# A graph network on one core: the segment maxima read their penalties from PSUM in pieces, and the adding transfers are shared out anew over the stages

## The chip, the cores and the metric

The kernel runs on one NeuronCore of one Trainium2 chip. The metric is the device time in microseconds (us) of one launch. Three runs of the kernel before took 6823.45, 6824.31 and 6814.25 us; their median is 6823.45 us.

The engines are named as in the profile: PE (TensorE matmul), PEld (its weight load), DVE (VectorE), ACT (ScalarE), POOL (GpSimd) and SP (SyncE, which here only issues transfers). A name with a q behind it (ACTq, SPq, POOLq, PEq) is that engine's sequencer.

## The reference, cut to what matters

The program is a stack of four graph layers on 6250 nodes and 106250 edges, sorted by target node. The first is a pair of attention convolutions (GATv2), the first with 8 heads of 16 channels and the second with 1 head of 64:

```
def _gatv2_layer(x, src, dst, Wl, bl, Wr, br, att, bias, heads, out_ch, concat):
    xl = (x @ Wl + bl).reshape(N, heads, out_ch)
    xr = (x @ Wr + br).reshape(N, heads, out_ch)
    e = jax.nn.leaky_relu(xl[src] + xr[dst], NEG_SLOPE)
    logits = jnp.einsum('ehc,hc->eh', e, att)
    m = jax.ops.segment_max(logits, dst, num_segments=N)
    ex = jnp.exp(logits - m[dst])
    denom = jax.ops.segment_sum(ex, dst, num_segments=N)
    alpha = ex / denom[dst]
    msg = xl[src] * alpha[..., None]
    out = jax.ops.segment_sum(msg, dst, num_segments=N)
...
_gatv2_layer(..., heads=8, out_ch=16, concat=True), then elu
_gatv2_layer(..., heads=1, out_ch=64, concat=False), then elu
```

The change touches `m`, the segment maxima of the two layers. The three layers behind (a normalised convolution, one with edge attributes and batch norms, and three more convolutions) are not changed. They read a dense adjacency matrix in DRAM, into which the kernel adds the edge weights while the two attention layers run.

## The kernel before, in words

**Stages.** The program is a row of stages. Each has all engines at work side by side and ends in a barrier of all engines (`S.end_stage()`, in the profile line L89): each engine drains, POOL collects the others, clears the semaphores and releases them. So a stage lasts as long as its slowest engine or transfer. An attention layer (`gat_layer`) has, in this order, the dense products (`two_dense`), the logits of all edges (`gat_logits`), the segment maxima (`edge_max`) and the weighted sums (`gat_sums`).

**Tiles.** The edges are cut into 880 tiles of 128 and these into 220 groups of 4. `gat_logits` writes the logits of every group to DRAM (`heads`), `edge_max` reads them all back, and `gat_sums` runs a software pipeline over the 220 groups.

**Segment maxima.** In `edge_max` the logits lie in one array `run` of 128 partitions by L columns, each partition with a consecutive stretch of edges (of one head, in layer 1): L is 7040 with 8 heads and 880 with one. A running maximum within each segment is one DVE scan, `state = max(state + penalty, value)`, where the penalty is 0 within a segment and -BIG where a new one starts. It is made forwards with the penalties `opens` and then backwards with `closes`, each time twice: once without what comes from the neighbouring partitions, then `carried` works out what crosses the partitions' borders (four small matmuls of PE and small DVE steps), and the scan is made again with it. The penalties are bf16 and lie in SBUF. ScalarE sums them once each (`sum_pens`), as `carried` needs the sum of each partition's penalties. Before that, `load_pens` has ScalarE's queue issue the loads: `opens` at once, and `closes` only after the first transfers of `opens` have landed and VectorE is through with `own_logits`, whose data lies where `closes` goes. `own_logits` is VectorE's work on the self loops, ahead of the scans. The results go back to DRAM in two transfers of SP, one for each half of the columns.

**Adding transfers.** `merge(groups)` is POOL's work beside the stages: for each of 150 groups of tiles, 4 indirect transfers that add edge weights into the adjacency matrix. Each of these transfers is one POOL instruction (DMA_INDIRECT, L1108). Two groups may be in flight: group n waits until group n-2 has landed, and where the blocks of both clash also until group n-1 has. Whether they clash is a number in the table `CLEAR`, which POOL's sequencer loads into a register ahead of each group (L1100). `MERGES` sets how many groups stand in which stage, for layer 1 and for layer 2: after the gathers of the logits, in the maxima, in the sums, and beside the work that follows. Each stage's barrier waits for all of its groups.

Of the kernel before, what the change touches and what calls it, by code (L numbers as in the profile page):

```python
# [7 lines left out]
ALU = mybir.AluOpType  # L8
ACT = mybir.ActivationFunctionType
# [10 lines left out]
P = 128  # L20
# [44 lines left out]
MERGES = ((2, 5, 64, 9), (2, 3, 54, 11))  # L65
# [65 lines left out]
def gnn(nc, A, out):  # L131
    S = Sems(nc)
    ve, ac, pe, po, sp = nc.vector, nc.scalar, nc.tensor, nc.gpsimd, nc.sync
    with ExitStack() as ctx:
# [958 lines left out]
        def merge(groups):  # L1093


            for n in range(sent[0], min(sent[0] + groups, FAR)):
                g, own, other = merge_turn(n), merged[n % 2], merged[(n + 1) % 2]
                wait(po, own, 16 * GT * (n // 2))
                if n > 2:
                    clear_at = nc.values_load(CLEAR[0:1, n - 1:n], engines=(POOL,), min_val=16 * GT,  # L1100
                                              max_val=16 * GT * FAR,
                                              skip_runtime_bounds_check_because="a count of transfers of groups")
                    po.wait_ge(other, clear_at)
                elif n:
                    po.wait_ge(other, 16 * GT)
# [841 lines left out]
        def edge_max(H, C, XL, XR, self_l):  # L1947
# [7 lines left out]
            assert L % 2 == 0  # L1955
            unread = G[:, :, :, :].rearrange("p r t d -> p (r t d)").bitcast(BF16)[:, 0:L // 2]
# [21 lines left out]
            sums_of_pens = [ends[:, 4 + i:5 + i] for i in range(4)]  # L1978
# [17 lines left out]
            def sum_pens():  # L1996

                ac.wait_ge(S("opens1"), 16 * H)
                for i, cols in enumerate(HALVES):
                    wait(ac, S("pens"), i)  # L2000
                    ac.activation(unread, opens[:, cols], ACT.Copy, accum_out=sums_of_pens[i]).then_inc(S("pens"), 1)
                ac.wait_ge(S("closes"), 16 * H)
                for i, cols in enumerate(HALVES):
                    ac.wait_ge(S("pens"), 2 + i)
                    ac.activation(unread, closes[:, cols], ACT.Copy, accum_out=sums_of_pens[2 + i]).then_inc(S("pens"), 1)

            def carried(flip):

                last = run[:, 0:1] if flip else run[:, L - 1:L]
                ve.wait_ge(S("pens"), 2 + 2 * flip)  # L2010
                go(ve, lambda: ve.tensor_tensor(ends[:, 1:2], sums_of_pens[2 * flip], sums_of_pens[2 * flip + 1], ALU.add))
# [3 lines left out]
                with ExitStack() as ps:  # L2015
                    lines = psum(ps, "lines", [P, 3 * P])
                    for n in range(2):
                        go(pe, lambda: pe.matmul(lines[0:1, n * P:(n + 1) * P], ends[:, n:n + 1], ident[:, :],
                                                 start=True, stop=True))
                    go(ve, lambda: ve.tensor_copy(row[0:1, 0:2 * P], lines[0:1, 0:2 * P]))  # L2020

                    start = chunks - 1 if flip else 0
                    first = [r.rearrange("a (h c) -> a h c", h=H)[:, :, start] for r in (penalty, carry)]
                    go(ve, lambda: ve.memset(first[0], -BIG))
                    turn = (lambda r: r[:, ::-1]) if flip else (lambda r: r)
                    go(ve, lambda: ve.tensor_tensor_scan(turn(state), turn(penalty), turn(value), -BIG,
                                                         ALU.add, ALU.max))
                    if flip:
                        go(ve, lambda: ve.tensor_copy(carry[:, 0:P - 1], state[:, 1:P]))
                    else:  # L2030
                        go(ve, lambda: ve.tensor_copy(carry[:, 1:P], state[:, 0:P - 1]))
                    go(ve, lambda: ve.memset(first[1], -BIG))
                    go(pe, lambda: pe.matmul(lines[:, 2 * P:2 * P + 1], carry, ones[0:1, 0:1], start=True, stop=True))
# [745 lines left out]
```

## Time and profile before

| | |
|---|---|
| median of 3 runs | 6823.45 us (6814.25 to 6824.31) |
| span of the profiled execution, first to last instruction | 6814.5 us |
| the profiled execution's own time | not given beside its span; the nearest run is 6814.25 us |
| POOL, DVE, PE, ACT busy | 68%, 55%, 82%, 32% of the span |
| L1108, adding transfers on POOL | 600 instructions, 1025.6 us busy |
| segment maxima of layer 1 | 1313.5 to 1417.8 us |
| sums of layer 1 | 1417.8 to 1921.5 us |
| segment maxima of layer 2 | 3158.3 to 3191.7 us |
| sums of layer 2 | 3191.7 to 3603.8 us |

Times within the trace count from the start of the span. A row of the timeline gives the start, the duration, the engine, the line, the operation with what it writes and reads, how many equal instructions it stands for, and in brackets how long the engine was idle before it and what ended that. A matmul's end is modelled; issuing, register, branch and semaphore instructions are not counted as busy. A stage's end is read off the first instruction of the next.

### The profile page before, as it was taken

To read this page: it belongs to the slowest core of one execution; us is meant where nothing else is said; L and a number is where in the kernel's file an instruction comes from. 1 tells how busy PE (TensorE), PEld (TensorE's weight loads), DVE (VectorE), ACT (ScalarE), POOL (GpSimd) and SP (SyncE) were. 2 spreads that over 40 slices of the span, in tenths; PEclk is the share of its full clock that TensorE was granted. 3 is DMA by queue.
4 is the path that set the end of the run, shared out by engine and by line. 5 is a ranking of instruction groups with operands and counts; after the bars stand their busy time and mean duration, and the time that the engine had idled before them with its cause. 6 is when DMAs were issued, how large, how long until landed. Compare 5 with 4: busy or idle time off the path is not lost. (4 is left out here: it accounts for less than half of the span.)

```text
span 6814.5 us, 123136 instructions
## 1 busy us (share of the span) xinstructions
PE 5620.4 (82%) x35774; PEld 4535.0 (67%) x35774; DVE 3761.5 (55%) x13008; ACT 2152.8 (32%) x6966; POOL 4663.4 (68%) x4391
## 2 busy tenths in 40 slices
PE   2999999557759999886886996666666599999999
PEld 2788888546657787775775996666666455555555
DVE  6555552389945555224887445666666544344343
ACT  4333334269923333333994003222222300000000
POOL 1777777688877777777887661777777267376473
PEclk9899999779969999997997998999999799999999
DMA  5888865656734444335444884555555389898997
GB/s 198 266 280 283 281 202 158 121 116 147 144 37 103 101 105 103 81 80 61 76 76 128 288 288 138 159 158 158 158 158 158 52 291 306 294 306 301 304 305 262
DMA packets 904054, 1232.19 MB, mean 181 GB/s; under 512 B 230601, under 2 KB 640861, under 8 KB 890407
## 3 DMA queue, kind: packets, MB, share of 16 engines
q1 hardware_dynamic: 607544, 887.00, 40.5%
q0 software_dynamic: 207392, 219.55, 17.6%
q10 hardware_dynamic: 88428, 117.57, 5.1%
q8 instruction: 295, 4.83, 0.3%
q14 instruction: 395, 3.24, 0.1%
HBM read 987.45 MB, written 237.38 MB: 180 GB/s over the span
## 5 line engine op out<-in xcount | busy, mean ns | idle before, releaser
L1024 POOL DMA_INDIRECT ACC<-table,TABS x1760 | 1701.3, 967 | 587.9 <-issue 583.3
L1346 POOL DMA_INDIRECT BUF<-table,TABS x840 | 797.5, 949 | 596.1 <-issue 245.4
L1108 POOL DMA_INDIRECT adjacency<-TABS x600 | 1025.6, 1709 | 247.8 <-issue 206.2
L1024 POOL DMA_INDIRECT BUF<-table,TABS x880 | 836.9, 951 | 331.3 <-issue 331.3
L1803 PE MATMUL picked<-ident,ACC 128*128 128x128 f32 (+1 forms) x3520 | 716.5, 287 | 0.0
L2169 PE MATMUL asum<-BUF 128*128 128x144 f32 x3520 | 544.5, 298 | 171.2 <-DVE BUF L2147 168.9
L1879 DVE SCALAR_TENSOR_TENSOR BUF<-BUF,TABS,wspread 128x128 bf16<-128x128 f32 (+1 forms) x600 | 323.9, 540 | 644.3 <-issue 625.6
L2169 PEld LDWEIGHTS asum<-BUF 128*128 128x128 f32 x3520 | 461.7, 192 | 202.4 <-issue 196.5
L2115 ACT ACTIVATE BUF<-iota_row,TABS 128x128 f32<-128x128 f32 x1760 | 555.1, 386 | 68.6 <-PEq L89 68.6
L1796 PE MATMUL picked<-ident 128*128 128x128 f32 x3520 | 565.2, 309 | 9.7 <-PEq L89 9.7
L1802 PE MATMUL picked<-G,OH 128*128 128x128 f32 (+1 forms) x2352 | 495.5, 295 | 84.3 <-DMA ACC<-table,TABS 70.1
L1718 PE MATMUL sums<-BUF,OH 128*128 128x128 f32 x1760 | 253.5, 288 | 361.9 <-DVE BUF L1704 361.8
L1796 PEld LDWEIGHTS picked<-ident 128*128 128x128 f32 x3520 | 475.5, 210 | 107.0 <-issue 106.8
L1823 PEld LDWEIGHTS lcol<-attT,BUF 128*128 128x128 f32 (+1 forms) x3520 | 433.2, 192 | 143.5 <-issue 141.6
L1803 PEld LDWEIGHTS picked<-ident,ACC 128*128 128x128 f32 (+1 forms) x3520 | 523.7, 177 | 0.0
L1054 DVE TENSOR_TENSOR ACC<-ACC,asum 128x144 f32 (+1 forms) x1760 | 462.1, 263 | 84.5 <-issue 10.1
L1829 ACT ACTIVATE ACC<-lcol 128x32 f32<-128x32 f32 (+1 forms) x440 | 81.7, 186 | 1281.0 <-PE lcol L1823 1267.8
L1718 PEld LDWEIGHTS sums<-BUF,OH 128*128 128x128 f32 x1760 | 217.6, 194 | 396.5 <-issue 396.4
L1823 PE MATMUL lcol<-attT,BUF 128*128 128x8 f32 (+1 forms) x3520 | 456.4, 252 | 2.7 <-ACT BUF L1841 2.7
L1815 DVE TENSOR_TENSOR BUF<-BUF,picked 128x512 f32<-128x512 f32 (+1 forms) x440 | 297.2, 676 | 230.8 <-ACT BUF L1809 230.7
L1802 PEld LDWEIGHTS picked<-G,OH 128*128 128x128 f32 (+1 forms) x2352 | 343.9, 178 | 118.4 <-issue 71.6
L1779 DVE TENSOR_SCALAR G<-BUF,iota_col 128x512 f32<-128x512 bf16 x440 | 219.2, 498 | 359.2 <-DMA BUF<-locals 355.1
(409 smaller groups left out, 10909.1 us busy)
## 6 DMA issues: line engine op xcount, KB each, us to landing
TABS<-adjacency SPq DMA_DIRECT2D x272, 512.0 KB
BUF<-in_edge_pair SPq DMA_DIRECT2D x880, 128.0 KB
BUF<-adjacency SPq DMA_DIRECT2D x102, 1024.0 KB
BUF<-adjacency SPq DMA_DIRECT2D x204, 512.0 KB, 5.1
adjacency<-zeros ACTq DMA_DIRECT2D x44, 1792.0 KB
G<-adjacency SPq DMA_DIRECT2D x136, 512.0 KB
kept<-ACC SPq DMA_DIRECT2D x220, 272.0 KB
G<-kept SPq DMA_DIRECT2D x220, 272.0 KB
```

The costliest lines, as they stand in the source:

```text
L1024: po.indirect_dma_start(rows[:, slot, j, 0:width], None, tab, bass.IndirectOffsetOnAxis(ap=SRC[:, q * GT + j:q * GT + j + 1], axis=0)).the ...
L1054: ve.tensor_tensor(at, at, self.from_[:, j, 0:self.width], ALU.add).then_inc(S("added"), 1)
L1108: po.indirect_dma_start(adj_flat, bass.IndirectOffsetOnAxis(ap=PLACE[:, k:k + 1], axis=0), TOTAL[:, k:k + 1], None, compute_op=ALU.add).th ...
L1346: po.indirect_dma_start(R[:, q % deep_ring, j, :], None, table, bass.IndirectOffsetOnAxis(ap=SRC[:, k:k + 1], axis=0)).then_inc(S(f"gather ...
L1718: m = pe.matmul(sums[h][:, j, :], OH[:, h, j, :], V[:, q % 3, j, :], start=True, stop=True)
L1796: pe.matmul(picked[slot][:, j * P:(j + 1) * P], ident[:, :], ident[:, :], start=True, stop=True)
L1802: pe.matmul(z, XRB[q % 3][:, j, :], OHT[:, slot, j, :], start=True, stop=False)
L1803: m = pe.matmul(z, R[:, q % DEEP, j, :], ident[:, :], start=False, stop=True)
L1823: m = pe.matmul(lcol[slot % 2][:, j * H:(j + 1) * H], Z[:, q % 3, j * P:(j + 1) * P], attT[0:W, 0:H], start=True, stop=True)
L1879: ve.scalar_tensor_tensor(JUNK[:, at % 3, 0:j + 1, :], KEYS[:, n % 2, 0:j + 1, :], KEY[:, k:k + 1], wspread[:, 0:j + 1, :], ALU.is_equal, ...
L2115: ac.activation(HOT[:, slot, j, :], iota_row[:, :], ACT.Abs, scale=-1.0, bias=LOCAL[:, bass.ds(q * GT + j, 1)]).then_inc(S("gap"), 1)
L2169: m = pe.matmul(sums[slot % 2][:, j, 0:WIDE], HOT[:, slot, j, :], RHS[:, slot, j, :], start=True, stop=True)
```

## The change

There are three parts.

1. `edge_max` no longer scans with penalties in SBUF. ScalarE copies them in pieces into PSUM (`put_pens`), two buffers in turn, and each DVE scan reads one piece there (`scans`). There are 5 pieces of 1408 columns with 8 heads and 2 of 440 with one. Every penalty is read in two passes, so there are 20 copies and 20 scans in layer 1, where 4 summing passes and 6 scans stood, and 8 and 8 in layer 2. The copies of the passes without the carried values give the sums too. The semaphore `scanned` counts scans, and `pens` counts copies: copy n waits for scan n-2, scan n for copy n and scan n-1.
2. `MERGES`: of the 80 groups of layer 1, 10 instead of 5 stand in the maxima and 59 instead of 64 in the sums. Of the 70 of layer 2, 4 instead of 3 stand in the maxima and 53 instead of 54 in the sums.
3. In `merge` the register load of `CLEAR` is no longer told to skip its bounds check.

The core of the diff:

```diff
-MERGES = ((2, 5, 64, 9), (2, 3, 54, 11))
+MERGES = ((2, 10, 59, 9), (2, 4, 53, 11))
...
                     clear_at = nc.values_load(CLEAR[0:1, n - 1:n], engines=(POOL,), min_val=16 * GT,
-                                              max_val=16 * GT * FAR,
-                                              skip_runtime_bounds_check_because="a count of transfers of groups")
+                                              max_val=16 * GT * FAR)
                     po.wait_ge(other, clear_at)
...
-            assert L % 2 == 0
-            unread = G[:, :, :, :].rearrange("p r t d -> p (r t d)").bitcast(BF16)[:, 0:L // 2]
+            pieces = 5 if H > 1 else 2
+            size, room = L // pieces, 3 * 512
+            assert L % 2 == 0 and L % pieces == 0 and size <= room
...
-            sums_of_pens = [ends[:, 4 + i:5 + i] for i in range(4)]
+            sums_of_pens = [ends[:, 4 + i * pieces:4 + (i + 1) * pieces] for i in range(2)]
+            turns = [(flip, full, k) for flip in (False, True) for full in (False, True)
+                     for k in (reversed(range(pieces)) if flip else range(pieces))]
...
-            def sum_pens():
-
-                ac.wait_ge(S("opens1"), 16 * H)
-                for i, cols in enumerate(HALVES):
-                    wait(ac, S("pens"), i)
-                    ac.activation(unread, opens[:, cols], ACT.Copy, accum_out=sums_of_pens[i]).then_inc(S("pens"), 1)
...
+            def put_pens(pens):
+
+                for n, (flip, full, k) in enumerate(turns):
+                    if flip:
+                        ac.wait_ge(S("closes"), 16 * H)
+                    else:
+                        ac.wait_ge(S(f"opens{((k + 1) * size - 1) // (L // 2)}"), 16 * H)
+                    wait(ac, S("scanned"), n - 1)
+                    given = (closes if flip else opens)[:, k * size:(k + 1) * size]
+                    more = {} if full else {"accum_out": sums_of_pens[flip][:, k:k + 1]}
+                    ac.activation(pens[:, n % 2, 0:size], given, ACT.Copy, **more).then_inc(S("pens"), 1)
...
+            def scans(pens, lines):
+
+                for n, (flip, full, k) in enumerate(turns):
+                    turn = (lambda t: t[:, ::-1]) if flip else (lambda t: t)
+                    at = slice(k * size, (k + 1) * size)
+                    data, pen = turn(run[:, at]), turn(pens[:, n % 2, 0:size])
...
+                    wait(ve, S("scanned"), n)
+                    ve.wait_ge(S("pens"), n + 1)
+                    if full and at_end:
+                        ve.wait_ge(chain[0].sem, chain[0].n)
+                    ve.tensor_tensor_scan(data, pen, data, initial, ALU.add, ALU.max).then_inc(S("scanned"), 1)
+                    if not full and k == (0 if flip else pieces - 1):
+                        ve.wait_ge(S("scanned"), n + 1)
+                        carried(flip, lines)
+                    if flip and full and at.start <= L // 2 < at.stop or flip and full and not k:
+                        half = 1 if k else 0
+                        sp.wait_ge(S("scanned"), n + 1)
+                        sp.dma_start(in_dram[:, HALVES[half]], run[:, HALVES[half]]).then_inc(S("maxima"), 16)
...
             load_pens()
-            sum_pens()
-            scans()
+            with ExitStack() as ps:
+                pens = psum(ps, "pens", [P, 2, room])
+                lines = psum(ps, "lines", [P, 3 * P])
+                put_pens(pens)
+                scans(pens, lines)
```

`carried` does what it did; its first step now sums 5 (or 2) columns of `sums_of_pens` instead of two.

Three places show how the instructions stand. The first is ScalarE in the maxima of layer 1, before, with the two loads ahead; `pool4` to `pool7` are semaphores, which stand for `opens0`, `opens1`, `closes` and `pens` there.

```order
L1993 DMA BUF<-close_pen 16x7040 [waits pool1,pool4]
L1993 DMA BUF<-close_pen 16x7040 x7
L2001 ACTIVATE G,st<-BUF 128x3520 [waits pool5]
L2001 ACTIVATE G,st<-BUF 128x3520 [waits pool7]
L2005 ACTIVATE G,st<-BUF 128x3520 [waits pool7,pool6]
L2005 ACTIVATE G,st<-BUF 128x3520 [waits pool7]
```

And now, where `pool7` is `scanned`:

```order
L1995 DMA BUF<-close_pen 16x7040 [waits pool1,pool4]
L1995 DMA BUF<-close_pen 16x7040 x7
L2008 ACTIVATE pens,st<-BUF 128x1408 [waits pool4] x2
L2008 ACTIVATE pens,st<-BUF 128x1408 [waits pool7,pool5] x3
L2008 ACTIVATE pens<-BUF 128x1408 [waits pool7,pool4] x2
L2008 ACTIVATE pens<-BUF 128x1408 [waits pool7,pool5] x3
L2008 ACTIVATE pens,st<-BUF 128x1408 [waits pool7,pool6] x5
L2008 ACTIVATE pens<-BUF 128x1408 [waits pool7,pool6] x5
```

The first copy stands behind the 8 loads of `closes`, and 20 copies stand where 4 passes stood.

The second is VectorE there, from the last step of `own_logits` to the second forward pass, before (a scan is called SCALAR_TENSOR_TENSOR in this listing):

```order
L1976 TENSOR_REDUCE st<-BUF 128x120 [waits pool1]
L2040 SCALAR_TENSOR_TENSOR ACC<-BUF,ACC 128x3520 [waits pool1,pool4,pool2]
L2040 SCALAR_TENSOR_TENSOR ACC<-BUF,ACC 128x3520 [waits pool1,pool5,pool3]
L2011 TENSOR_TENSOR st<-st 128x1 [waits pool1,pool7]
L2012 COPY st<-ACC 128x1 [waits pool1]
```

And now, where `pool8` is the new `pens`:

```order
L2053 SCALAR_TENSOR_TENSOR ACC<-pens,ACC 128x1408 [waits pool8,pool2]
L2053 SCALAR_TENSOR_TENSOR ACC<-pens,ACC 128x1408 [waits pool8,pool7,pool2]
L2053 SCALAR_TENSOR_TENSOR ACC<-pens,ACC 128x1408 [waits pool8,pool7,pool3] x3
L2013 TENSOR_REDUCE st<-st 128x1 [waits pool1,pool7]
L2014 COPY st<-ACC 128x1 [waits pool1]
```

Each scan now waits for a copy of ScalarE, the first one included.

The third is POOL at the start of the maxima of layer 1, two of its groups before (L89 is the barrier):

```order
L89 ISA [waits barrier_Pool_Activation_PE_DVE_SP_gather]
L1108 DMA adjacency<-TABS 37748736x1 [waits merged_into_adjacency_0,merged_into_adjacency_1]
L1108 DMA adjacency<-TABS 37748736x1 x3
L1100 TENSOR_LOAD CLEAR [waits merged_into_adjacency_1]
L1108 DMA adjacency<-TABS 37748736x1 [waits merged_into_adjacency_0]
L1108 DMA adjacency<-TABS 37748736x1 x3
```

And now:

```order
L89 ISA [waits barrier_Pool_Activation_PE_DVE_SP_gather]
L1107 DMA adjacency<-TABS 37748736x1 [waits merged_into_adjacency_0,merged_into_adjacency_1]
L1107 DMA adjacency<-TABS 37748736x1 x3
L1100 TENSOR_LOAD CLEAR [waits merged_into_adjacency_1]
L1100 ISA x2
L1107 DMA adjacency<-TABS 37748736x1 [waits merged_into_adjacency_0]
L1107 DMA adjacency<-TABS 37748736x1 x3
```

Behind each of the 147 loads of `CLEAR` there are now two instructions of POOL's sequencer (ISA x2, asserts of the lower and upper bound) that were not there.

## Rows read from the trace of the kernel before

**Rows 1.** The page: busy time by engine, and the group of layer 1's gathers
```profile
PE 5620.4 (82%) x35774; PEld 4535.0 (67%) x35774; DVE 3761.5 (55%) x13008; ACT 2152.8 (32%) x6966; POOL 4663.4 (68%) x4391
L1024 POOL DMA_INDIRECT ACC<-table,TABS x1760 | 1701.3, 967 | 587.9 <-issue 583.3
```
**Rows 2.** Windows, the four stages: length, busy (count) by engine, PE clock, DMA share, GB/s
```profile
1313.50:1417.80 104.30, 3.50 (x12) 1.33 (x12) 91.15 (x34) 12.92 (x8) 86.81 (x20) 0.50 0.49 104
1417.80:1921.50 503.70, 349.80 (x2200) 299.07 (x2200) 431.61 (x1761) 422.82 (x1321) 420.02 (x256) 0.94 0.65 131
3158.30:3191.70 33.40, 3.50 (x12) 1.33 (x12) 25.50 (x26) 2.65 (x9) 25.16 (x12) 0.50 0.27 41
3191.70:3603.80 412.10, 338.58 (x2200) 293.63 (x2200) 342.08 (x1982) 402.71 (x1320) 338.21 (x216) 0.99 0.48 74
```
**Rows 3.** Timeline, end of layer 1's sums
```profile
1880.31 1.64 DVE L1054 TENSOR_TENSOR ACC<-ACC,asum 128x144 f32 x4 [0.23 <-DVE ACC L1054]
1881.13 1.55 POOL L1108 DMA_INDIRECT adjacency<-TABS  x1 [0.31 <-issue]
...
1916.44 1.55 POOL L1108 DMA_INDIRECT adjacency<-TABS  x1 [0.30 <-issue]
1921.51 0.56 DVE L2223 TENSOR_SCALAR st<-ACC 128x392 f32<-128x392 f32 x1 [39.56 <-PEq L89]
```
**Rows 4.** Timeline, end of layer 2's sums
```profile
3595.36 1.57 POOL L1108 DMA_INDIRECT adjacency<-TABS  x1 [0.31 <-issue]
...
3600.59 1.32 DVE L1054 TENSOR_TENSOR ACC<-ACC,asum 128x67 f32 x4 [0.31 <-DVE ACC L1054]
3603.84 0.21 DVE L2223 TENSOR_SCALAR st<-ACC 128x49 f32<-128x49 f32 x1 [1.93 <-PEq L89]
```
**Rows 5.** Timeline, layer 1's maxima
```profile
1338.99 2.17 POOL L1108 DMA_INDIRECT adjacency<-TABS  x1 [5.01 <-DMA adjacency<-TABS]
...
1342.00 3.61 ACTq L1993 DMA_DIRECT2D BUF<-close_pen  x8
1342.05 15.18 DVE L2040 TENSOR_TENSOR_SCAN ACC<-BUF,ACC 128x3520 f32<-128x3520 bf16 x2
1343.32 7.58 POOL L1108 DMA_INDIRECT adjacency<-TABS  x1 [0.30 <-issue]
1345.65 3.14 ACT L2001 ACTIVATE G<-BUF 128x3520 bf16<-128x3520 bf16 x1 [35.98 <-issue]
...
1361.22 14.88 DVE L2043 TENSOR_TENSOR_SCAN ACC<-BUF,st,ACC 128x7040 f32<-128x7040 bf16 x1
1362.61 14.86 POOL L1108 DMA_INDIRECT adjacency<-TABS  x1 [0.30 <-issue]
...
1402.62 7.55 DVE L2049 TENSOR_TENSOR_SCAN ACC<-BUF,ACC 128x3520 f32<-128x3520 bf16 x1
1404.25 7.28 POOL L1108 DMA_INDIRECT adjacency<-TABS  x1 [0.30 <-issue]
```
**Rows 6.** Timeline, layer 2's maxima
```profile
3172.31 1.55 POOL L1108 DMA_INDIRECT adjacency<-TABS  x1 [0.30 <-issue]
3172.63 0.57 ACT L2001 ACTIVATE G<-BUF 128x440 bf16<-128x440 bf16 x1 [16.21 <-DVE st L1976]
...
3186.34 1.57 POOL L1108 DMA_INDIRECT adjacency<-TABS  x1 [0.31 <-issue]
...
3187.94 1.13 DVE L2049 TENSOR_TENSOR_SCAN ACC<-BUF,ACC 128x440 f32<-128x440 bf16 x1
```
**Rows 7.** Timeline, layer 1's logits: a DVE operation that reads PSUM, and POOL
```profile
1267.48 0.67 DVE L1815 TENSOR_TENSOR BUF<-BUF,picked 128x512 f32<-128x512 f32 x1
1267.61 0.94 POOL L1024 DMA_INDIRECT ACC<-table,TABS  x1 [0.30 <-issue]
```
**Rows 8.** The same operation with both inputs in SBUF (layer 2's dense products)
```profile
1968.35 0.69 DVE L885 TENSOR_TENSOR BUF<-BUF 128x512 f32<-128x512 f32 x1
```
**Rows 9.** Line L1100: count, shortest/median/longest in ns
```profile
L1100 POOLq TENSOR_LOAD <-CLEAR x147: 283/288/309, 1315.3 to 3674.5; - x147
```

More of the change, by code:

```diff
@@ L2014, in carried @@
                 state, carry = row[0:1, 2 * P:3 * P], st[2][0:1, 0:P]
[L2015 to L2029, printed above, removed]
-                    else:
-                        go(ve, lambda: ve.tensor_copy(carry[:, 1:P], state[:, 0:P - 1]))
-                    go(ve, lambda: ve.memset(first[1], -BIG))
-                    go(pe, lambda: pe.matmul(lines[:, 2 * P:2 * P + 1], carry, ones[0:1, 0:1], start=True, stop=True))
-                    go(ve, lambda: ve.tensor_copy(ends[:, 2:3], lines[:, 2 * P:2 * P + 1]))
@@ L2036, in scans @@
-            def scans():
-                for i, cols in enumerate(HALVES):
-                    ve.wait_ge(S(f"run{i}"), 16)
-                    ve.wait_ge(S(f"opens{i}"), 16 * H)
-                    go(ve, lambda: ve.tensor_tensor_scan(run[:, cols], opens[:, cols], run[:, cols],
-                                                         run[:, L // 2 - 1:L // 2] if i else -BIG, ALU.add, ALU.max))
-                carried(False)
-                go(ve, lambda: ve.tensor_tensor_scan(run, opens, run, ends[:, 2:3], ALU.add, ALU.max))
-                ve.wait_ge(S("closes"), 16 * H)
-                go(ve, lambda: ve.tensor_tensor_scan(run[:, ::-1], closes[:, ::-1], run[:, ::-1], -BIG, ALU.add, ALU.max))
-                carried(True)
-                for i in (1, 0):
-                    data, pen = (t[:, HALVES[i]][:, ::-1] for t in (run, closes))
-                    go(ve, lambda: ve.tensor_tensor_scan(data, pen, data, ends[:, 2:3] if i else run[:, L // 2:L // 2 + 1],
-                                                         ALU.add, ALU.max))
-                    sp.wait_ge(chain[0].sem, chain[0].n)
-                    sp.dma_start(in_dram[:, HALVES[i]], run[:, HALVES[i]]).then_inc(S("maxima"), 16)
@@ new lines, in carried @@
+                for n in range(2):
+                    go(pe, lambda: pe.matmul(lines[0:1, n * P:(n + 1) * P], ends[:, n:n + 1], ident[:, :],
+                                             start=True, stop=True))
+                go(ve, lambda: ve.tensor_copy(row[0:1, 0:2 * P], lines[0:1, 0:2 * P]))
+                start = chunks - 1 if flip else 0
+                first = [r.rearrange("a (h c) -> a h c", h=H)[:, :, start] for r in (penalty, carry)]
+                go(ve, lambda: ve.memset(first[0], -BIG))
```

25 lines of the change are left out of this document (18 added, 7 removed).

## The prediction

> **What bounds the kernel now.** I read the page first. POOL is busy 68% of the span and PE 82% [rows 1], but the kernel is a row of stages with a barrier behind each, so shares decide nothing. I went on to the windows of the four stages that the change touches [rows 2], then to the timeline at each one's end, to see who is last there.
>
> Sums of layer 1, 503.7 us: DVE's last add ends at 1880.31 + 1.64 = 1881.95, PE's matmuls are done before it, and POOL goes on alone with adding transfers, one every 1.86 us, until 1916.44 + 1.55 = 1917.99. DVE sits idle for 39.56 us [rows 3]. POOL bounds this stage. From POOL's last end to the next stage it is 1921.51 - 1917.99 = 3.5 us.
>
> Sums of layer 2, 412.1 us: POOL's last transfer ends at 3596.93 and DVE's last add at 3601.91; the next stage starts 1.9 us after DVE [rows 4]. The pipeline bounds it. POOL with its 3.5 us would have been through at 3600.4, so it has 3.4 us of slack.
>
> Maxima of layer 1, 104.3 us: a chain of DVE. The scans end at 1402.62 + 7.55 = 1410.17 [rows 5], and the last result transfer and the barrier take the 7.6 us to 1417.8. In it POOL does 20 transfers only: a transfer started beside a scan takes 7.58, 14.86 and 7.28 us instead of 1.55, and ends 1.4 us after the scan does (1362.61 + 14.86 = 1377.47 against 1376.10) [rows 5]. The scans shut it out. Maxima of layer 2, 33.4 us: DVE ends at 3189.07, POOL at 3187.91 [rows 6], next stage 3191.7.
>
> **Part 1, the groups taken from layer 1's sums.** 5 groups are 20 transfers. The last 20 began at 1881.13 (the 18 left out in rows 3 repeat the pattern), so the 236 that stay would end at 1880.8, and POOL would let the barrier go at 1880.8 + 3.5 = 1884.3. The pipeline would do so at 1881.95 + 1.9 = 1883.9. The two are level, and what is late next is both. The stage shrinks from 503.7 to 466.5 us: **-37.2 us**. The pace over the whole stage gives the same: 256 transfers in 500.2 us are 1.95 each, and 236 of them 461, to 1879.
>
> **Part 2, scans by pieces in layer 1.** Three terms on DVE's chain.
> (a) The first scan began at 1342.05, just behind own_logits. Now it needs a copy, and ScalarE first issues 8 loads of closes, which hold it until 1345.65 [rows 5]. ScalarE takes 3.14 us for 3520 columns and 0.57 for 440 [rows 5, 6], so 0.834 ns a column and 0.20 fixed: 1.38 us for 1408. With some 0.15 for reading out the sum and for the semaphore the scan starts at 1347.2: **+5.1**.
> (b) A scan takes 7.55 us for 3520 columns and 1.13 for 440, so 2.085 ns a column and 0.21 fixed: 3.15 for 1408. 20 of them with about 0.12 between (two scans with a wait between take 15.18, not 15.10; those with waits on two further semaphores a little more) are 65.3 us. The six of before took 68.12 less the two carried steps of 4.0 = 60.1. **+5.2**. The copy (1.5) lies beside the scan before it (3.15), since two buffers are there. closes, issued by 1345.6, is first needed at about 1380, 34 us later; opens, as large, was there 28 us after its issue.
> (c) The barrier: POOL's last transfer ended at 1404.25 + 7.28 = 1411.53, and with it in the way the next stage came 7.6 us behind the scans. POOL is now done earlier; I take **-1** for it.
> Together **+9.3 us**, if POOL gets through its 40 transfers. It has begun 10 before 1343.32 (that row is its eleventh) as before; the other 30 at 1.95 take 58.5 us, to 1402. The loads of opens delayed a landing until 1338.99, a stall of 5.01 [rows 5]; closes, as large, may cost such a stall again: 1407. The scans end at 1420.5 and the next stage starts at 1427.1; POOL, with its 3.5, may take until 1423.6. There are 17 us of cover.
>
> **Does a scan with one input in PSUM leave POOL alone?** Rows 7: L1815 reads PSUM and SBUF, POOL's transfer starts 0.13 us into it with 0.54 to go, and takes 0.94. Shut out, it would have taken 0.54 and then, as behind the scans, 1.4. Over all 1760 gathers the mean is 0.967 [rows 1], though an L1815 of 0.68 runs beside every few of them, so hardly one was held. I take it that such a scan does leave POOL alone.
> The Trainium skill says the same as a mechanism (SBUF — State Buffer, "SBUF: two separate sides"): VectorE and GpSimd share one pair of ports, an exclusive lock that a DVE operation takes with two SBUF inputs or in a two-port mode and holds to its end. The scans of before agree (14.86 us beside 14.88).
>
> **What a PSUM read costs.** The trace has no scan from PSUM. The nearest rows: 128x512 with PSUM takes 0.67 and with both in SBUF 0.69 [rows 7, 8]. I take no difference for the 28 scans; the lower end is no gain either.
> A rule speaks against it: the Trainium skill (VectorE: DVE Perf Modes, "The TRN2 errata") has VectorE's fixed part at 120 cycles from PSUM against 58 from SBUF, which by its 0.96 GHz is an estimate of 0.065 us a scan, 1.3 us for 20. Rows 7 and 8 do not show it.
> The upper end is a copy that doesn't lie beside its scan: 1.5 us for each of 19 further pieces, +28.5 (rival C).
>
> **Part 3, layer 2's maxima.** On DVE, the first copy starts at 3172.63 [rows 6] and the scan at 3173.35, 1.05 later; 8 scans of 1.13 + 0.12 are 10.0 against 8.85 (3172.30 to 3189.07 less two carried steps): +2.2, which would have the next stage at 3193.9. POOL has 16 transfers instead of 12. The fifth began at 3172.31, and 12 at 1.86 from there end at 3194.3; with the 3.5 us of rows 3 behind them the next stage starts at 3197.8. POOL becomes the last: 3197.8 - 3191.7 = **+6.1 us**. (Before, 12 transfers ended at 3187.91, and DVE's scans held some of them: 8 took 15.6 us instead of 14.9.)
>
> **Part 4, layer 2's sums.** One group fewer on POOL, which isn't the bound: **0**. The 9 and 11 groups behind the sums stay.
>
> **Part 5, the asserts.** 147 pairs on POOL's sequencer. A CLEAR load (0.288 us) [rows 9] stands ahead of each group too, and every gap between transfers is 0.30 us [rows 3], a group's first or not: the sequencer works ahead of the engine. Taken at 0. Above: each assert as long as that load and not hidden, 0.58 us a group.
>
> **The sum** against the execution's span: -37.2 + 9.3 + 6.1 + 0 = -21.8, 6814.5 to 6792.7. The span is level with the fastest run (6814.25) and 9 us under the median, and the difference is what carries over: 6823.45 - 21.8 = **6801.7 us**.
>
> **Rivals.**
> A. The scans go on shutting POOL out (the port is held all the same). For: POOL's stretched transfers [rows 5] say nothing of the reason. Against: rows 7. Then one transfer goes with each scan: 10 + 20 + 4 in the carried steps = 34 by the end of the scans at 1420.5, and 6 more at 1.86 with the 1.4 behind the scan and the drain end the stage at 1436, 18.2 over before. Layer 2's maxima, with a transfer or two held, about +7.5. -37.2 + 18.2 + 7.5 = -11.5: 6812 us.
> B. The asserts are not hidden, and the kernel gets slower. Place: POOL's queue ahead of each group. At 0.58 us a pair: layer 1's sums +34.2 on a POOL-bound stage, layer 2's maxima +2.3, layer 2's sums 53 x 0.58 = 30.7 less the slack, which is 3.4 and the group taken away, 7.4: +19.9. In all +56.4 - 21.8 = +34.6: 6858 us. With p us a pair it is 116 p - 10.8 - 21.8: it eats the gain from 0.28 us a pair, and shows as slower from 0.40. Against it: the gaps of rows 3.
> C. The hand-over between ScalarE and VectorE is serial (PSUM can't be written and read at once, or the semaphores cost more than I think). Layer 1 +28.5; layer 2's scans 7 x 0.67 = 4.7, of which POOL hides all but 0.8. +29.3 - 21.8 = +7.5: 6831 us. For: nothing in this trace has ScalarE write PSUM while VectorE reads it. Against: they use different parts of PSUM, and PE writes PSUM while DVE reads in every pipeline here.
>
> **How the numbers follow.** Forecast 0.74, A 0.08, B 0.06, C 0.12. A measurement of this kernel tells about 0.2% (13.6 us) from no change: below 6809.8 is faster, above 6837.1 slower. The forecast's own spread is some 9 us (stalls for landings in the maxima, the pace in the sums, which of the runs' levels from 6814 to 6824 holds), so nearly all of it is faster. C is the same at full price and in part faster; A just so. Faster 0.78, same 0.15, slower 0.07. The range runs from 6788, below the forecast, to 6816, which takes in A and the cheaper part of C.
>
> **What would show it.** Right: in the sums of layer 1 DVE's idle time before L2234 (the old L2223) falls from 39.56 to under 5 us; the stage is 466 us. In layer 1's maxima 40 transfers of POOL, those beside the scans at 1.55 to 2 us; 20 scans of 3.15; the first at 5 us behind own_logits; a stage of 113 to 114 us. In layer 2's maxima POOL is last, 39.5 us. Gaps between transfers stay 0.30. Wrong: transfers of 3 us beside the scans (A), gaps of 0.6 or more ahead of each group's first transfer (B), scans 4.5 us apart (C).

## The result, and the profile after

The changed kernel takes 6811.51 us (median of 20 runs, 6798.93 to 6826.45) against 6823.66 us of the kernel before (20 runs, 6812.41 to 6836.07). The ratio is 0.9983, 95% interval 0.9978 to 0.9989: 11.6 us less, with 7.5 and 15.0 as ends (the two medians differ by 12.2). Forecast were 21.8 us less, 6801.7 us. The direction and the place were right, and the size was half of what I forecast.

The profiled execution took 6799.69 us for a span of 6797.9, so the launch adds 1.8 us to a span. It is the second fastest of the 20. The windows of the same four stages as in [rows 2], with the same columns:

```profile
1317.50:1429.50 112.00, 3.50 (x12) 1.33 (x12) 94.17 (x48) 28.05 (x30) 67.31 (x40) 0.50 0.53 97
1429.50:1899.40 469.90, 357.07 (x2200) 305.78 (x2200) 432.40 (x1761) 422.84 (x1321) 387.29 (x236) 0.95 0.71 140
3134.00:3172.80 38.80, 3.51 (x12) 1.33 (x12) 25.88 (x28) 4.71 (x13) 30.18 (x16) 0.50 0.29 35
3172.80:3584.70 411.90, 341.19 (x2200) 296.06 (x2200) 341.27 (x1982) 402.87 (x1320) 331.85 (x212) 0.98 0.50 74
```

They are 1032.6 us against 1053.5, so 20.9 less: +7.7, -33.8, +5.4, -0.2. The forecast had +9.3, -37.2, +6.1 and 0.

The end of layer 1's sums, where [rows 3] had DVE idle for 39.56 us (L2234 is the old L2223, L1107 the old L1108):

```profile
1889.55 1.55 POOL L1107 DMA_INDIRECT adjacency<-TABS  x1 [0.30 <-issue]
...
1897.09 1.65 DVE L1054 TENSOR_TENSOR ACC<-ACC,asum 128x144 f32 x4 [0.23 <-DVE ACC L1054]
...
1899.51 0.56 DVE L2234 TENSOR_SCALAR st<-ACC 128x392 f32<-128x392 f32 x1 [0.77 <-PEq L89]
```

POOL is through at 1891.10 and DVE at 1898.74. The pipeline bounds the stage now, and the 36 us that POOL had for itself are gone.

Layer 1's maxima, the stretch that answers to [rows 5]:

```profile
1343.83 2.15 DVE L1976 TENSOR_REDUCE st<-BUF 128x120 f32<-128x1920 f32 x1
...
1346.07 3.61 ACTq L1995 DMA_DIRECT2D BUF<-close_pen  x8
...
1349.73 1.35 ACT L2008 ACTIVATE pens<-BUF 128x1408 f32<-128x1408 bf16 x1 [35.97 <-issue]
1349.75 1.55 POOL L1107 DMA_INDIRECT adjacency<-TABS  x1 [0.30 <-issue]
...
1351.30 16.06 DVE L2053 TENSOR_TENSOR_SCAN ACC<-pens,ACC 128x1408 f32<-128x1408 f32 x5 [5.31 <-ACT pens L2008]
1351.61 1.55 POOL L1107 DMA_INDIRECT adjacency<-TABS  x1 [0.30 <-issue]
...
1371.38 3.15 DVE L2053 TENSOR_TENSOR_SCAN ACC<-pens,st,ACC 128x1408 f32<-128x1408 f32 x1
...
1374.62 28.74 DVE L2053 TENSOR_TENSOR_SCAN ACC<-pens,ACC 128x1408 f32<-128x1408 f32 x9
1374.62 1.35 ACT L2008 ACTIVATE pens<-BUF 128x1408 f32<-128x1408 bf16 x1 [5.83 <-DVE ACC L2053]
1374.72 1.55 POOL L1107 DMA_INDIRECT adjacency<-TABS  x1 [0.31 <-issue]
...
1406.31 1.55 POOL L1107 DMA_INDIRECT adjacency<-TABS  x1 [0.31 <-issue]
...
1407.38 3.15 DVE L2053 TENSOR_TENSOR_SCAN ACC<-pens,st,ACC 128x1408 f32<-128x1408 f32 x1
1410.57 12.71 DVE L2053 TENSOR_TENSOR_SCAN ACC<-pens,ACC 128x1408 f32<-128x1408 f32 x4
```

Three things are to be seen. The first scan waits 5.31 us for the first copy, which stands behind the 8 loads of closes. Nine scans take 28.74 us, 3.19 each with the hand-over, and each later copy (1.35) lies beside a scan. POOL's transfers take 1.55 us in the middle of scans and follow each other at 1.86; the last of the 40 ends at 1407.86, 21.6 us ahead of the next stage.

In layer 2's maxima POOL is last:

```profile
3165.13 1.13 DVE L2053 TENSOR_TENSOR_SCAN ACC<-pens,ACC 128x440 f32<-128x440 f32 x1
...
3168.46 1.57 POOL L1107 DMA_INDIRECT adjacency<-TABS  x1 [0.30 <-issue]
3172.79 0.40 ACT L2126 ACTIVATE BUF<-iota_row,TABS 128x128 f32<-128x128 f32 x1 [12.20 <-PEq L89]
```

The line of the bounds check shows what the asserts are:

```profile
L1100 POOLq TENSOR_LOAD <-CLEAR x147: 283/288/306, 1319.4 to 3655.4; - x147
L1100 POOLq FUSED_REGOPS  x147: 147/147/181, 1319.7 to 3655.7; - x147
L1100 POOLq SEQ_ASSERT  x147: 18/18/28, 1320.0 to 3655.9; - x147
```

Each group costs POOL's sequencer 0.165 us more (0.147 and 0.018), while the gaps between transfers stay at 0.30.

### The profile page after: what moved, and what is told of

It reads as the page before. It is cut to its first block and busy times, and to the rows that moved or that the text cites. A ratio compares the mean times of both kernels' runs of the same rounds, so it can differ in the third digit from the quotient of the medians.

```text
span 6797.9 us, 123518 instructions
## 1 busy us (share of the span) xinstructions
PE 5630.2 (83%) x35774; PEld 4544.0 (67%) x35774; DVE 3768.0 (55%) x13024; ACT 2169.8 (32%) x6992; POOL 4606.4 (68%) x4391
## 3 DMA queue, kind: packets, MB, share of 16 engines
q0 software_dynamic: 207392, 219.55, 18.4%
## 5 line engine op out<-in xcount | busy, mean ns | idle before, releaser
L1107 POOL DMA_INDIRECT adjacency<-TABS x600 | 971.7, 1619 | 285.3 <-issue 242.4
```

The source lines that it names most:

```text
L1107: po.indirect_dma_start(adj_flat, bass.IndirectOffsetOnAxis(ap=PLACE[:, k:k + 1], axis=0), TOTAL[:, k:k + 1], None, compute_op=ALU.add).th ...
```

## The experiments

The runs fell into three batches, each on one chip and with its own runs of the kernel before. On the chips of batch 1 and batch 3 this kernel is slower: the kernel before takes 8391.83 and 8353.17 us there (medians), and the mean granted clock is 0.821 to 0.830 in the profiled executions, where it was 0.935 for [rows 2]. Batch 2 was on a chip like the first (6815.58 us). Across the chips the maxima repeat to some 0.4 us and layer 2's sums to 2, so they can be compared; layer 1's sums move by up to 11 us for one and the same kernel. The time of the slower chips goes into stages that the change doesn't touch, above all the logits. A ratio is always against the kernel before in the same batch. All lengths, from barrier to barrier in us:

```
                         maxima 1  sums 1  maxima 2  sums 2 |  four   | logits 1
before                    104.31   503.67   33.35    412.12 | 1053.45 | 1141.01
after                     111.99   469.93   38.80    411.89 | 1032.61 | 1146.08
asserts_again (batch 2)   104.33   502.54   33.36    412.90 | 1053.13 | 1139.60
padded (batch 2)          104.01   503.60   33.35    411.88 | 1052.84 | 1140.48
sbuf_pieces (batch 2)     118.48   472.13   40.71    410.97 | 1042.29 | 1139.93
best (batch 2)            106.90   470.71   33.57    411.95 | 1023.13 | 1143.33
asserts_only (batch 1)    104.38   497.60   33.37    412.18 | 1047.53 | 1632.27
scans_only (batch 1)      112.16   494.49   35.28    411.61 | 1053.54 | 1652.04
merges_only (batch 1)     139.19   476.27   40.49    410.99 | 1066.94 | 1635.05
a_again (batch 1)         111.99   480.68   38.81    411.01 | 1042.49 | 1656.02
a_third (batch 3)         111.99   472.52   38.82    411.00 | 1034.33 | 1628.10
scans_again (batch 3)     111.99   498.86   34.90    412.04 | 1057.79 | 1635.39
early_copies (batch 3)    106.79   480.54   38.84    412.64 | 1038.81 | 1640.36
```

**asserts_only.** The kernel before with part 3 of the change alone.

```diff
-                                              max_val=16 * GT * FAR,
-                                              skip_runtime_bounds_check_because="a count of transfers of groups")
+                                              max_val=16 * GT * FAR)
```

> The kernel before with the bounds check of the register load (part 3 alone). My theory (hidden, since POOL's sequencer works ahead of the engine): gaps between transfers stay 0.30 us, the four stages last 104, 504, 33 and 412 us, whole kernel 0 +- 3 us. Rival (an assert costs as the load before it, 0.29 us, twice and not hidden): layer 1's sums 504 + 64 x 0.58 = 541 us and the whole kernel 50 us slower.

Measured: ratio 1.0005 (0.9990 to 1.0019), with the maxima and layer 2's sums of the old lengths. Layer 1's sums take 497.60 us, 6 less than before and not more. The gap ahead of a group's first transfer there is 0.30 us (median), as between the others. The asserts are hidden; rival B is out.

**scans_only.** The changed kernel with the old groups.

```diff
-MERGES = ((2, 10, 59, 9), (2, 4, 53, 11))
+MERGES = ((2, 5, 64, 9), (2, 3, 54, 11))
```

> The changed scans and asserts with the old shares of adding transfers (5, 64, 9 and 3, 54, 11). My theory (only the moved transfers gain, and the scans cost): layer 1's maxima 112 us (+7.7), POOL idle in them early; layer 1's sums stay bound by POOL at 504 us; layer 2's maxima bound by VectorE at 35.5 us (+2.2). Whole kernel +10 us, 6833. Rival (the scans from PSUM gain by themselves, as scan and POOL no longer hold each other up): no more than the time of before, 6823 or less.

Measured: 1.0012 (0.9998 to 1.0025). The maxima are 112.16 and 35.28 us: the scans by pieces cost 7.8 and 1.9 us and bring nothing by themselves. Layer 1's sums are 494.49 us, not the 504 expected, and POOL is last there still (see below).

**merges_only.** The kernel before with parts 2 and 3.

```diff
-MERGES = ((2, 5, 64, 9), (2, 3, 54, 11))
+MERGES = ((2, 10, 59, 9), (2, 4, 53, 11))
```

> The old scans with both inputs in SBUF, with the new shares of adding transfers (10, 59 and 4, 53) and the asserts. My theory (the scans shut POOL out): layer 1's maxima hold 20 further transfers that start only behind the scans, 20 x 1.86 us and 3.5 us to the next stage: about 139 us (+34); the sums 469 us (-34); layer 2's maxima 39.5 us (+6). Whole kernel +6 us, 6830. Rival (the shares alone make the gain, and POOL finds room in the stage anyway): layer 1's maxima 105 us, whole kernel 6795 to 6800.

Measured: slower, 1.0022 (1.0006 to 1.0038), 18 us (5 to 32) where 6 were expected. The maxima came as expected, 139.19 us; layer 1's sums are 476.27 instead of 469. The window and POOL's last transfer of that stage:

```profile
1806.07:1945.26 139.19, 3.50 (x12) 1.33 (x12) 91.16 (x34) 12.92 (x8) 116.80 (x40) 0.50 0.43 78
```
```profile
1940.25 1.55 POOL L1107 DMA_INDIRECT adjacency<-TABS  x1 [0.30 <-issue]
1945.76 0.40 ACT L2114 ACTIVATE BUF<-iota_row,TABS 128x128 f32<-128x128 f32 x1 [88.21 <-PEq L89]
```

POOL works on to 1941.8, long after the scans, which had shut it out. What the sums give back (21.3 us against asserts_only) is more than eaten. So the new groups don't pay beside the long scans of before, and the scans by pieces don't pay without the new groups.

**a_again.** The changed kernel unchanged, in the same batch.

> The changed kernel once more, unchanged, for a second trace of it. Theory N (what the four changed stages gain is fixed, and the rest of the difference to the whole program's time is drift of stages that the change doesn't touch, with the phase of TensorE's clock): the four stages last 112, 470, 38.8 and 412 us again within 2 us each, some 21 us less than before in sum, while the untouched stages move by up to 5 us each in either direction between traces. Theory S (the change itself makes other stages slower): the layer 1 logits last 1146 us again as in the first trace of the changed kernel, 5 us more than before. Whole kernel: ratio 0.998.

Measured: 0.9992 (0.9981 to 1.0003), 6.7 us less, which is not clear of no change. The maxima repeat to 0.01 us. The sums of layer 1 do not, against the expectation of 470 within 2: 480.68 us.

**sbuf_pieces.** The pieces and groups of the changed kernel, but ScalarE copies the penalties to SBUF (into G, as bf16).

```diff
-                pens = psum(ps, "pens", [P, 2, room])
+                pens = G[:, :, :, :].rearrange("p r t d -> p (r t d)").bitcast(BF16)[:, 0:2 * size].rearrange(
+                    "p (a n) -> p a n", a=2)
```

> The changed kernel, with ScalarE's pieces written as bf16 into SBUF instead of f32 into PSUM: the same 20 copies and 20 scans, the same shares of transfers, but both inputs of a scan in SBUF. My theory (it is the place of the penalties that frees POOL): a transfer begun beside a scan lasts to the scan's end, one goes with each scan, 34 of 40 are through when the scans end, and 6 more at 1.86 us end layer 1's maxima at about 122 us; layer 2's at 40 us. Rival (short scans with gaps between are enough to let POOL through): 112 and 38.8 us as in the changed kernel. The scans themselves 3.15 us in both, if a read from PSUM costs nothing more.

```profile
1342.95 1.55 POOL L1107 DMA_INDIRECT adjacency<-TABS  x1 [0.30 <-issue]
...
1344.38 16.06 DVE L2053 TENSOR_TENSOR_SCAN ACC<-G,ACC 128x1408 f32<-128x1408 bf16 x5 [5.31 <-ACT G L2008]
1344.81 4.02 POOL L1107 DMA_INDIRECT adjacency<-TABS  x1 [0.30 <-issue]
...
1349.13 2.94 POOL L1107 DMA_INDIRECT adjacency<-TABS  x1 [0.30 <-issue]
...
1352.38 2.94 POOL L1107 DMA_INDIRECT adjacency<-TABS  x1 [0.30 <-issue]
```

What changed is where the penalties lie, and with it their type (bf16, as before the change, instead of f32). The scans take the same (five in 16.06 us, as from PSUM), and POOL's transfers beside them take some 2.9 us, and one 4.02, instead of 1.55: about one for each scan. 35 of the 40 are through when the scans end; 34 were expected. Maxima 118.48 us instead of 111.99. Two findings: a scan with both inputs in SBUF holds POOL up and one with an input in PSUM doesn't, and reading PSUM costs the scan nothing.

Ratio 0.9984 (0.9975 to 0.9993), which the timed runs can't tell from the changed kernel's 0.9983. So cutting the scans is what turns the loss of merges_only into a gain, since a transfer gets in between two pieces: 139.19 us become 118.48. PSUM brings the other 6.5 us in layer 1's maxima and 1.9 in layer 2's (40.71 to 38.80), seen in the stages alone. Not tested is a kernel that cuts the scans and reads the penalties where they lie, without any copy. It would have no first copy to wait for.

The Trainium skill (VectorE: DVE Perf Modes, "The TRN2 errata") would make the 20 scans from PSUM 1.3 us longer, an estimate from its fixed cycles; the two rows of 16.06 us do not show it. Its rule on the shared ports (SBUF — State Buffer, "SBUF: two separate sides") is borne out as far as VectorE holds POOL up: with two SBUF inputs it does, with one it doesn't. The other direction, POOL's transfer holding up a scan, is not to be seen here: the transfers of 2.94 us end 1.27 us into the next scan, and that scan still takes 3.15 us.

**best.** The changed kernel with ScalarE's first two copies issued ahead of the loads of closes, and layer 2's groups put back.

```diff
-MERGES = ((2, 10, 59, 9), (2, 4, 53, 11))
+MERGES = ((2, 10, 59, 9), (2, 3, 54, 11))
...
-            def load_pens():
+            def load_pens(pens):
...
+                put_pens(pens, 0, 2)
...
-                for n, (flip, full, k) in enumerate(turns):
+                for n, (flip, full, k) in list(enumerate(turns))[first:last]:
...
-                put_pens(pens)
+                load_pens(pens)
+                put_pens(pens, 2, len(turns))
```

> The changed kernel with two edits: ScalarE makes its first two copies before it issues the loads of closes, and layer 2 has its old shares (3 and 54). My theory (the first scan's 5.1 us wait is the queue of ScalarE, and in layer 2's maxima the fourth group makes POOL the last): VectorE's first scan starts right behind own_logits; layer 1's maxima 112 - 5.1 = 107 us; layer 2's 35.3 - 1.05 = 34.2 us; the sums as they were, 412 us in layer 2. The four stages 9.7 us less than in the changed kernel. Rival (closes is then late, or copies during own_logits hold its operations): layer 1's maxima stay at 110 us or more.

```profile
1335.56 1.35 ACT L2009 ACTIVATE pens<-BUF 128x1408 f32<-128x1408 bf16 x1 [24.09 <-DMA BUF<-open_pen]
...
1341.57 2.15 DVE L1976 TENSOR_REDUCE st<-BUF 128x120 f32<-128x1920 f32 x1
1343.32 1.55 POOL L1107 DMA_INDIRECT adjacency<-TABS  x1 [0.31 <-issue]
1343.63 16.05 DVE L2054 TENSOR_TENSOR_SCAN ACC<-pens,ACC 128x1408 f32<-128x1408 f32 x5
1343.81 3.61 ACTq L1996 DMA_DIRECT2D BUF<-close_pen  x8
```

Measured: 6786.08 us (6779.82 to 6795.90, 5 runs), ratio 0.9955 (0.9941 to 0.9968). The first scan starts as soon as own_logits is done. The four stages are 30.3 us shorter than before, and the time is 30.7 us less. Its interval lies below the changed kernel's (0.9978 to 0.9989), so this kernel beats both.

**asserts_again and padded.** They test whether the length and place of the instruction stream moves the stages that the change doesn't touch. The first is asserts_only once more; the second adds to it, in the maxima of both layers together, 20 tiny copies on ScalarE and 16 on VectorE, as many as the change adds copies and scans there.

```diff
+            for i in range(16 if H > 1 else 4):
+                ac.wait_ge(chain[0].sem, chain[0].n)
+                ac.activation(ends[:, 20 + i:21 + i], ends[:, 4:5], ACT.Copy)
+            for i in range(14 if H > 1 else 2):
+                ve.wait_ge(chain[0].sem, chain[0].n)
+                ve.tensor_copy(ends[:, 50 + i:51 + i], ends[:, 4:5])
```

> asserts_only again, for a second trace of it on the chip of these runs: it says how far an untouched stage moves by itself. Theory R (chance): layer 1's logits differ from the first trace's by as much as the kernels differed among each other, 10 us and more. Theory P: 1632 to 1636 us again on a chip like the second one, the old length. Maxima 104.4 and 33.4 us, layer 1's sums 497 to 504 us.

> asserts_only with 20 tiny ScalarE and 16 tiny VectorE copies behind the scans (16 and 14 in layer 1, 4 and 2 in layer 2), which compute nothing: the program is as long as the changed one on these engines, with the old scans and shares. It asks why stages that the change doesn't touch came out longer with the new scans (layer 1's logits 1146, 1656, 1652 us against 1141, 1632, 1635 with the old). Theory P (how long or where the instruction streams are sets it): on a chip like the second one layer 1's logits last 1650 us or more here, 15 to 20 us over a kernel of the old length on the same chip. Theory R (chance): within the 1632 to 1636 of the old scans, or scattered. The maxima 1 to 3 us longer than in asserts_only.

Measured: 1.0002 (0.9993 to 1.0011) and 0.9998 (0.9989 to 1.0007), logits of layer 1 1139.60 and 1140.48 us. No sign that the longer stream costs anything.

**a_third, scans_again, early_copies.** The changed kernel and scans_only once more, and best with the changed kernel's groups. They ask whether kernels with penalties in PSUM have longer logits, and what the early copies bring alone.

> The changed kernel, unchanged, once more. Question: its four changed stages gave 20.9 us in the traces, the timed runs gave 11.6 us (7.5 to 15.0). Theory N (the untouched stages differ by a few us from one execution to the next and from one batch of runs to the next): the changed stages are 20 to 22 us shorter than the 1053.4 of the kernel before again, the time comes out 11 to 21 us below the kernel before, and layer 1's logits, 1146.1 us in the first trace, fall anywhere between 1139 and 1147. Theory L (kernels whose penalties lie in PSUM have a longer stage of logits, by a cause not known): layer 1's logits are 1143 to 1147 us again, against 1139.6 to 1141.0 of the kernels with scans from SBUF, and the time is 11 to 16 us below the kernel before.

> The scans from PSUM and the asserts alone, with the groups as before. By my sum: layer 1's maxima +7.7 (112 us), layer 2's maxima +1.9 (35.3), the sums unchanged (503 and 412), so the changed stages are 1063 us, +9.6 on the kernel before; slower by 0.14% (ratio 1.0014). Theory N: layer 1's logits 1139 to 1147, no pattern. Theory L: logits 1143 to 1147, and the ratio 1.0017 to 1.0021.

> The changed kernel with one thing moved: ScalarE's first two copies are issued ahead of the 8 loads of closes instead of behind them; the groups stay as the change has them. By my account of the maxima the first scan follows own_logits at once: layer 1's maxima 107 us (112.0 in the changed kernel), layer 2's maxima 38.8 us as in the changed kernel, since POOL is last there. The changed stages are 5 us shorter than the changed kernel's 1032.6, near 1027.6. The rival: the first copies are not what the first scan waits for, and layer 1's maxima stay at 112.

Measured: 0.9988 (0.9975 to 1.0001), 1.0007 (0.9993 to 1.0021) and 0.9961 (0.9945 to 0.9977). The early copies give 5.2 us in the maxima (106.79), as expected, so the first copies are what the first scan waited for. Batch 3 has no kernel without penalties in PSUM, so its logits (1628.10, 1635.39 and 1640.36 us) can't decide on Theory L. In batch 1 they are 1652.04 and 1656.02 us with and 1632.27 and 1635.05 without, on one chip. But which execution was profiled goes along with that: the profiled ones of asserts_only and merges_only were 19.5 and 9.7 us below the medians of their kernels, those of scans_only and a_again 6.0 and 12.5 above. The medians follow the four stages: against asserts_only the stages of scans_only, merges_only and a_again are 6.0 longer, 19.4 longer and 5.0 shorter, and the medians 7.1 more, 18.4 more and 4.7 less. Logits longer by 20 us in every execution would stand out there; 5 us might not.

## Why the prediction was right, and where its size was off

**Layer 1's sums: -33.8 instead of -37.2.** POOL did what I had worked out: its 236 transfers end 461.6 us into the stage, and I had 463. What I had level with it was the pipeline, taken over from the trace of before as ending 464.15 us into the stage. It ended at 469.2, and the barrier came 0.8 us behind it instead of 1.9. The windows of the stage's start and of its main part, before:

```profile
1417.80:1433.20 15.40, 8.49 (x31) 7.47 (x32) 11.07 (x24) 10.41 (x31) 12.20 (x8) 0.50 0.61 122
1417.80:1880.00 462.20, 349.80 (x2200) 299.07 (x2200) 430.32 (x1757) 422.82 (x1321) 388.12 (x236) 0.97 0.69 142
```

and after:

```profile
1429.50:1451.00 21.50, 14.55 (x53) 12.84 (x54) 15.60 (x42) 14.83 (x45) 17.11 (x11) 0.51 0.67 125
1429.50:1890.00 460.50, 352.94 (x2174) 302.39 (x2174) 425.26 (x1735) 420.64 (x1315) 386.19 (x236) 0.95 0.72 143
```

TensorE starts the stage at 0.50, its lower level of 1.2 GHz, after the idle maxima, and rose 15 us into the stage before and 21 us after. Later it falls back for some microseconds at a time. Up to the pipeline's end it spent 26 us at the lower level before and 43 after, so the later start of the higher level is 6 us of these 17. Its clock over the main part is 0.95 instead of 0.97. In the kernel before that would have cost nothing, because POOL was last. Three further traces of the new groups show that the stage's length now goes with the clock (a_third, a_again, early_copies, in this order):

```profile
1910.67:2383.19 472.52, 358.52 (x2200) 307.18 (x2200) 433.00 (x1761) 422.87 (x1321) 386.61 (x236) 0.95 0.69 139
```
```profile
1938.57:2419.24 480.67, 370.05 (x2200) 317.90 (x2200) 433.98 (x1761) 422.77 (x1321) 382.70 (x236) 0.93 0.70 137
```
```profile
1918.27:2398.81 480.54, 372.24 (x2200) 319.82 (x2200) 433.64 (x1761) 422.85 (x1321) 383.97 (x236) 0.92 0.68 137
```

The seven traces of the new groups form one row: 469.9, 470.7, 472.1 and 472.5 us at a clock of 0.95, 476.3 at 0.94, and 480.7 and 480.5 at 0.93 and 0.92. The last four of these (a_third, merges_only, a_again, early_copies) are from the slower chips.

The old groups show the same row, once the pipeline's end (VectorE's last add) is read and not the stage's. All times are counted from the barrier at the stage's start; the clock is that up to the pipeline's end:

```
                clock  pipeline's end  POOL's end  stage   POOL busy with transfers
before          0.972      464.3         500.4     503.67    420.0
asserts_again   0.958      468.8         499.3     502.54    418.4
padded          0.951      472.2         500.3     503.60    418.1
scans_again     0.942      475.2         495.5     498.86    414.6
asserts_only    0.937      476.1         494.3     497.60    413.8
scans_only      0.894      488.8         491.4     494.49    410.7
after           0.955      469.4         461.7     469.93    387.3
```

So the trace that I took 464.15 from has the highest clock and the shortest pipeline of all thirteen, the slower chips or not: on the chip of batch 2, with the old groups, it ended at 468.8 and 472.2. With it PE's busy time grows for the same 2200 matmuls, from 349.8 us (before) to 384.3 (scans_only). That the two go together is shown; a cause that moves both is not ruled out. POOL's end moves the other way: its gaps are the same (79 to 81 us in each), and its transfers take up to 9.3 us less in sum where the pipeline is slower. Why they do was not followed.

This part of the gain was 30 to 34 us in every pair of traces of the fast chips and 14 to 26 on the slower ones. My -37.2 took the pipeline's end from one execution as fixed, and by chance from the most favourable one. I set a bound free that moves with the clock, and gave it one value.

**Layer 1's maxima: +7.7 instead of +9.3.** (a) The first scan stands 33.8 us into the stage instead of 28.55: +5.25 for my +5.1. (b) From its start to the end of the last scan (1423.28) are 71.98 us; less two carried steps of 4.02 that is 63.9 for 20 scans, 3.20 each. I had 65.3: 3.15 a scan was right, and the hand-over is 0.05 us, not 0.12. +3.8 instead of +5.2. (c) The next stage came 6.2 us behind the scans instead of 7.6: -1.4 for my -1. POOL's cover of 17 us was 18.1 by the same reckoning (the 21.6 above less the 3.5 to the next stage).

**Layer 2's maxima: +5.4 instead of +6.1.** POOL's last end came 36.0 us into the stage, as worked out. The next stage came 2.8 us behind it, not 3.5. Best, with 12 transfers there again, has 33.57 us.

**Layer 2's sums and the asserts: 0.** -0.2, and three kernels that differ from the old time by less than can be measured.

**The rivals.** A needed transfers that go with each scan: they are there with penalties in SBUF, not in PSUM. B needed gaps ahead of the groups: none. C needed scans 4.5 us apart: 3.20. None of them has a share in the missing part. But the time alone would not have told: A came to 6812 us, and 6811.51 was measured. That is chance. Where A's mechanism is really there, in sbuf_pieces, the stages gain 11.2 us, and A had 11.5. And 6811.51 lies above the 6809.8 below which I called a kernel faster; only 20 runs on each side make the interval narrow enough to be clear of no change.

**From 20.9 to 11.6 us.** The step of the prediction that failed by most is none of the stages: it is that the difference of two profiled executions carries over to the medians. The missing 9.3 us are 4.3 in the rest of the program, 4.4 between the spans and the medians, and 0.6 between the medians' difference and the ratio. The changed stages are 20.9 shorter, the spans 16.6 (6814.5 to 6797.9). The rest of the program was thus 4.3 us longer, and layer 1's logits alone 5.1 (1146.08 against 1141.01). Over the six traces of the fast chips this rest runs from 5761.1 to 5768.9 us (after 5765.3), and here too the old trace is the shortest. The medians differ by 12.2 and not by 16.6: the profiled execution of the changed kernel, at a clock of 0.937 where its 20 runs had 0.929 to 0.937, lies 11.8 us below its own median. With its 1.8 us the old profile's 6814.5 is only 7.4 below. Whether an average run of the changed kernel has longer sums than the profiled one can't be read, since only profiled runs show stages; the profiled execution of sbuf_pieces is that kernel's median (6806.05) and has 472.1 us there, only 2.2 more, so I don't expect the rest in that stage.

What stays open: in batch 2 the ratio of sbuf_pieces (10.9 us less for stages 11.2 shorter) and of best (30.7 for 30.3) match their stages, and only the changed kernel falls short of its own. Early_copies is off to the other side: 32.6 us less (19.2 to 45.9), where its stages explain about 13 (the changed kernel's 6.7 to 10.0 and 5.2). Longer logits with penalties in PSUM would explain the first and not the second. In the traces of the fast chips they are 1146.08 and 1143.33 with PSUM and 1139.60 to 1141.01 without, two against four, and in batch 1 the order is the same; but there the medians speak against it, and best, which has them too, does not fall short. So Theory L is neither shown nor ruled out for a few microseconds.

## What to carry to other kernels

Where a GpSimd queue of transfers and long VectorE operations with two SBUF inputs share a stage, cut the operations into pieces and put one input into PSUM. Here 20 more transfers made the kernel slower beside the long scans (1.0022). They made it faster beside pieces from SBUF (0.9984), and PSUM gave the stage another 6.5 us, since no transfer was held up beside a scan any more. The price was 7.7 us in that stage, so it pays only where the transfers that move were the last work of another stage. When you take the last engine out of a stage, the next one sets its end, and if that is TensorE's pipeline, the gain is a range and not one number from one profile, because that pipeline's time moves with the granted clock (464 to 489 us for clocks of 0.97 to 0.89 here). Put the first short operation of a chain ahead of a row of DMA issues on its own queue: behind 8 issues that take 3.6 us, the first copy was the largest term of the cost in layer 1's maxima (5.25 of 7.7 us), and moving two copies took it back.

## What I had not expected of the hardware

- A scan of 1408 columns takes 3.15 us with the penalties as f32 in PSUM and as bf16 in SBUF alike, and the hand-over from ScalarE through a semaphore adds 0.03 to 0.09 us, 0.05 on average, when two buffers are there.
- ScalarE's copy of 1408 columns takes 1.35 us into PSUM and 1.38 us into SBUF, and 0.19 us more for reading out the sum.
- The changed kernel takes 6811.51 us in the runs of the result and 8387.88 in batch 1. No chip was used in two batches, so what the chip does and what the hour does are not told apart. Layer 1's maxima are 112.0 us in both. Layer 1's logits are 1146.08 and 1656.02 us, with a granted clock of 0.92 and 0.76 and DMA rates of 230 and 159 GB/s (first the one, then the other):

```profile
171.00:1317.00 1146.00, 1080.39 (x7640) 941.64 (x7640) 547.78 (x1724) 408.59 (x1540) 851.32 (x888) 0.92 0.79 230
```
```profile
170.56:1826.58 1656.02, 1298.48 (x7640) 1118.56 (x7640) 542.21 (x1724) 396.86 (x1540) 849.13 (x888) 0.76 0.54 159
```

PE is busy for 218 us more, which is not enough for the 510, and DVE, ACT and POOL are busy no longer than in the first. What the stage waits for there I have not followed.
